# Cross-attention and feed-forward, two layers: four stages run into one another

## What is computed

```
x = x + xattn0(layernorm(x), ctx)          # attention over channels, 32 rows a head
x = x + ffn0(layernorm(x), 4-bit weights)  # silu(gate) * up, down, then y / rms(y)
x = x + xattn1(layernorm(x), ctx)          # 16 heads of 32, below
x = x + ffn1(layernorm(x))                 # ternary weights, gelu between

xattn1: q = x @ Wq + bq;  k, v = split(ctx @ Wkv + bkv)
        q, k, v rounded to 127 steps of their maxima (q, k per row and head, v per column)
        p = softmax(q k^T) over all 2048 keys, rounded to 255 steps of its row maximum
        out = (p v) @ Wp + bp
```

## Time and profile before

| | us |
|---|---|
| median of 3 runs | 1866.02 |
| lowest, highest | 1864.51, 1867.11 |
| the profiled execution | 1868.98 |
| its span in the trace | 1867.2 |

### The profile page before, as it was taken

How to read it: one execution, slowest core, us unless ns; L and a number is a source line. 1 busy time by engine, 2 the same in 40 slices (tenths; PEclk the granted TensorE clock), 3 DMA queues, 4 the chain that set the end, 5 groups by cost and what they waited for, 6 DMA issues and landing times. The chain is left out here.

```text
span 1867.2 us, 30272 instructions
## 1 busy us (share of the span) xinstructions
PE 1699.0 (91%) x10553; PEld 747.7 (40%) x10706; DVE 1494.4 (80%) x2799; ACT 1248.7 (67%) x2107; POOL 907.1 (49%) x927
## 2 busy tenths in 40 slices
PE   3999999689999977989799999999999997999999
PEld 0333233134444433434244444444444444444444
DVE  5899999876867664877699999999999995884332
ACT  4888888445544431223399999999999995774333
POOL 5667665355445420000088888888888884000000
PEclk8999999889999998999899999999999998999999
DMA  9856551301011005556455555655666667110220
GB/s 203 224 147 139 143 145 29 105 11 23 1 23 23 1 6 175 101 101 116 89 108 108 109 109 108 113 109 114 114 114 106 105 108 229 31 23 27 42 45 23
DMA packets 421687, 170.45 MB, mean 91 GB/s; under 512 B 382112, under 2 KB 392352, under 8 KB 420384
## 3 DMA queue, kind: packets, MB, share of 16 engines
q1 hardware_dynamic: 421536, 168.51, 41.8%
HBM read 69.89 MB, written 4.19 MB: 40 GB/s over the span
## 5 line engine op out<-in xcount | busy, mean ns | idle before, releaser
L1586 ACT ACTIVATE a_prob<-a_psS,a_bias,q_scale 128x1024 uint8<-128x1024 f32 x512 | 610.7, 1210 | 25.5 <-PE a_psS L1479 20.5
L1515 DVE TENSOR_REDUCE a_tops<-a_psM 128x1 f32<-128x512 f32 x1024 | 622.7, 681 | 2.0 <-PE a_psM L1469 0.6
L1565 POOL CAST a_wide<-a_pairs 128x2048 int16<-128x2048 uint8 x256 | 481.4, 1891 | 96.9 <-DMA a_pairs<-a_prob 87.8
L1469 PE MATMUL a_psM<-KT,QO 128*128 128x512 bf16 x969 | 354.0, 387 | 21.9 <-DVE a_tops L1515 10.5
L1479 PE MATMUL a_psS<-KT,QO 128*128 128x512 bf16 x966 | 292.6, 380 | 6.7 <-ACT a_prob L1586 3.7
L1491 PEld LDWEIGHTS a_psO<-V,a_wide 128*128 128x128 f16 x4096 | 174.9, 96 | 144.9 <-DVE QO L1528 23.0
L1491 PE MATMUL a_psO<-V,a_wide 128*128 128x32 bf16 x4096 | 181.3, 177 | 20.4 <-DVE QO L1528 15.6
L843 DVE SCALAR_TENSOR_TENSOR g_sum<-g_psG,gu_scale,g_sum 128x512 f32<-128x512 f32 x176 | 124.2, 746 | 89.8 <-PE g_psG L995 75.0
L821 POOL TENSOR_TENSOR g_sum<-g_sum 128x512 f32<-128x512 f32 x88 | 126.3, 1435 | 140.4 <-DVE g_sum L843 140.4
L478 ACT ACTIVATE prob<-psT 128x512 f32<-128x512 f32 x256 | 142.9, 599 | 63.8 <-remote 32.0
L942 ACT ACTIVATE g_sum<-g_psG,gu_scale 128x512 f32<-128x512 f32 x176 | 111.2, 681 | 109.9 <-PE g_psG L995 109.0
(11 more groups left out here) (212 smaller groups left out, 2737.5 us busy)
## 6 DMA issues: line engine op xcount, KB each, us to landing
xs<-in_x SPq DMA_DIRECT2D x64, 256.0 KB, 6.2
cs<-in_ctx SPq DMA_DIRECT2D x64, 256.0 KB, 8.3
KT<-in_w SPq DMA_DIRECT2D x2, 4096.0 KB, 19.1
raw_gu<-in_gu SPq DMA_DIRECT2D x4, 1408.0 KB, 8.1
vs<-in_ctxT SPq DMA_DIRECT2D x16, 256.0 KB, 2.9
QO<-in_ctxT SPq DMA_DIRECT2D x4, 1024.0 KB, 11.3
a_pairs<-a_prob SPq DMA_TRANSPOSE x256, 2.7
out<-x_sb SPq DMA_DIRECT2D x16, 256.0 KB, 2.2
```

The lines of the kernel that those rows point to most:

```text
L1469: pe.matmul(psM[n % NM][:, :], QOf[:, i * P:(i + 1) * P], KTf[:, keys:keys + 512], start=True, stop=True).then_inc(shown, 1)
L1515: v.reduce_max(tops[i // JOIN % NB][:, i % JOIN, c:c + 1], psM[n % NM][:, :], AX.X).then_inc(topped, 1)
L1565: pool.tensor_copy(wide[i % NV][:, :, :, :].rearrange("p k c q -> p k (c q)"), both).then_inc(widened, 1)
L1586: act.activation(prob[i % NP][:, k * HK:(k + 1) * HK], psS[g % NS][:, :], ACT.Exp, scale=q_scale[:, i:i + 1], bias=bias[i // JOIN % NB][:, ...
```

## The change

The gated stage and the keys, values and queries become one block, and so do the attention and the projection with what follows; between these two blocks all engines still meet. Within a block each engine goes on to the next stage's program when its own is through, and waits on semaphores guard memory and banks that are used again.

- A tile `early` of 7 x 512 words a partition takes the first context piece, the value weights of groups 0 and 1, and the key bias. SP issues these three behind the gated stage's transposes. All else it issues after the gated stage's last product, row and copy. The tile later holds the projection's `o` and `oT`.
- The ring of the keys has three banks (NA = 3). `bias_rows(0)` comes first on VectorE, `bias_rows(1)` after value unit 5, the normaliser after unit 7. ScalarE loads its table at the start of this stage.
- From query tile 8 on, TensorE makes two `show` products after each query tile and VectorE takes two maxima, so that the 16 of the first four steps are made in the query stage. Attention's own programs start behind them.
- The factor 1/sqrt(32) is taken into each query tile's operations; the operation on all of q_scale and the one that negates it are gone, and GpSimd negates in its second small operation.
- SP no longer waits for the turned tiles; GpSimd does so before its first `offset`, and TensorE before the tiles it reads.
- In attention `psM` moves behind `psS` and `psO` in PSUM (banks 5 to 7 instead of 0 to 2), and the maxima with what is made of them lie in one tile of 28 words a partition.
- TensorE transposes and projects tiles 0 and 1 between the last four `weigh` steps. VectorE inverts 15 tiles' sums and divides before it copies the last head's result (`keep_last`, after the update of tile 0). The ternary weights are issued when the last score is made.

```diff
+        ffn = gated_ffn(env, dn_in, dns_in)
+        keys = keys_values_queries(env, ctxT_in, wkv_in, bkv_in, bv_in, wq_in, bq_in, ahead)
+        with nc.Block() as block:
+            @block.sync
+            def _(sp):
+                ffn.sync(sp)
+                keys.sync(sp)
...
+        with nc.Block() as block:
+            @block.sync
+            def _(sp):
+                attended.sync(sp)
+                rest.sync(sp)
...
-    NA = 4
-    AHEAD = 4
+    NA, AHEAD, FIRST_SHOWN = 3, 4, 8
...
-            sp.dma_start(bv[:, :], bv_in).then_inc(loaded[0], 16)
-            fetch_wv(0, 0)
+            fetch_wv(wv_first, 0, 0)
             fetch_ctx(0, 0)
-            fetch_wv(1, 1)
+            sp.dma_start(raw[0], bkv_in[0:DM].partition_broadcast(P)).then_inc(loaded[5], 16)
+            for done in ("products", "rows", "taken"):
+                sp.wait_ge(*env["ffn_done"][done])
+            sp.dma_start(bv[:, :], bv_in).then_inc(loaded[1], 16)
             fetch_ctx(1, 2)
...
-            sp.wait_ge(v_turned, 16 * CH)
-            for b in range(2):
-                sp.wait_ge(turned[b], 16 * NT)
...
-            normaliser(v, env)
+            bias_rows(0)
             for kind, i in ORDER:
                 if kind == "v":
                     values(i)
-                    if i == 1:
-                        bias_rows(0)
-                    if i == 3:
+                    if i == 5:
+                        v.wait_ge(b_own, 5)
                         bias_rows(1)
                         v.wait_ge(b_own, 10)
+                    if i == 7:
+                        v.wait_ge(*env["ffn_done"]["stats"])
+                        normaliser(v, env)
...
                     if i + 4 < NT:
                         normalise(i + 4)
+                    if i >= FIRST_SHOWN:
+                        for n in (2 * (i - FIRST_SHOWN), 2 * (i - FIRST_SHOWN) + 1):
+                            piece(v, n // CH, n % CH)
...
+                    if i == FIRST_SHOWN:
+                        pe.wait_ge(turned[0], 16 * (NT // 2 + 1))
+                        pe.wait_ge(turned[1], 16 * NT // 2)
+                    if i >= FIRST_SHOWN:
+                        for n in (2 * (i - FIRST_SHOWN), 2 * (i - FIRST_SHOWN) + 1):
+                            show(pe, n // CH, n % CH)
...
-            for i in range(AHEAD):
-                for c in range(PIECES):
-                    show(i, c)
...
+                if i >= N:
+                    turn(pe, i - N)
...
-            pool.wait_ge(negated, 1)
+            for b in range(2):
+                pool.wait_ge(env["keys_done"]["turned"][b], 16 * NT)
...
+        def turn(pe, i):
+            if i == 0:
+                pe.wait_ge(*env["attended"]["topped"])
+                transpose(pe, 0)
+                transpose(pe, 1)
+            if i == 1:
+                pe.wait_ge(w_in, 16 * (CH + 1))
+                pe.wait_ge(env["attended"]["exped"], 2 * H1 * NT)
+            if i in (1, 2):
+                project(pe, i - 1)
+                transpose(pe, i + 1)
...
+            sp.wait_ge(*env["attended"]["scored"])
             for i, (w_dram, n) in enumerate(((w1_in, FF), (w2_in, DM))):
...
+            v.wait_ge(attended["exped"], 2 * H1 * (NT - 1))
+            v.wait_ge(attended["o_read"][0], NT - 1)
             invert(own, 0, 2)
             divide(0)
             divide(1)
-            invert(own, 2, NT)
+            invert(own, 2, NT - 1)
...
+                if t == 1:
+                    keep_last()
+                    v.wait_ge(attended["exped"], 2 * H1 * NT)
+                    invert(own, NT - 1, NT)
```

More of the change, by code:

```diff
@@ L1 @@
+from collections import namedtuple
 from contextlib import ExitStack
@@ L142, in build @@
         env["w_sums"] = sb("w_sums", [P, 2 * WS], F32)
[L143 to L155, removed]
+        env["V"] = sb("V", [P, NT, H1, D1], BF16)
@@ new lines, in build @@
+        env["v_scale"] = sb("v_scale", [P, CH], F32)
+        env["QO"] = sb("QO", [P, NT * H1, P], BF16)
+        env["q_scale"] = sb("q_scale", [P, NT * H1], F32)
+        env["maxima"] = sb("maxima", [P, 28], F32)
+        env["wp_loaded"] = env["sems"].enter_context(nc.semaphore("wp_loaded"))
+        with ExitStack() as later:
+            env["e_sum"] = later.enter_context(nc.sbuf_tensor("e_sum", [P, NT * H1 * 2], F32))
+            rest, turn = project_and_ternary(env, w1_in, w2_in, b1_in, b2_in, out)
+            attended, ahead = attend(env, wp_in, bp_in, turn)
@@ L779, in gated_ffn @@
              "squared", "own", "added", "after"))
-        block = ctx.enter_context(nc.Block())
+        env["ffn_done"] = dict(products=(y_done, NT), rows=(added, NT), stats=(after_s, NT), taken=(y_taken, NT))
         SIDES = (0, 1)
@@ L1162, in _, with gpsimd @@
                     turn_queries(i)
-            sp.wait_ge(v_turned, 16 * CH)
-            for b in range(2):
-                sp.wait_ge(turned[b], 16 * NT)
-        @block.gpsimd
-        def _(pool):
+        def gpsimd(pool):
+            for done in ("products", "rows", "taken"):
+                pool.wait_ge(*env["ffn_done"][done])
             pool.memset(ones_b[:, :], 1.0).then_inc(blank, 1)
@@ L1353, in keys @@
                 for i in range(CH):
-                    pe.matmul(out[:, :], cT[:, i, t * P:(t + 1) * P], wkv[:, i, 0:DM], start=(i == 0), stop=False)
+                    pe.matmul(out[:, :], context(t // TPC)[:, i, t % TPC * P:(t % TPC + 1) * P], wkv[:, i, 0:DM], start=(i == 0), stop=False)
                 pe.matmul(out[:, :], ones_b[:, :], rows[0][:, :], start=False, stop=True).then_inc(k_done, 1)
@@ L1436, in attend, with show, join, piece @@
         spare = QO[:, :, :].rearrange("p (t h) n -> p t (h n)", h=H1)[:, :, 2 * DM:]
+        env["psO"] = psO
+        env["attended"] = dict(exped=exped, weighed=weighed, topped=(topped, N * PIECES), o_read=(o_read, NT),
+                               scored=(scored, 2 * N))
+        def show(pe, i, c):
+            n = PIECES * i + c
+            if n >= NM:
+                pe.wait_ge(topped, n - NM + 1)
+            keys = (i % H1) * TOK + c * 512
+            pe.matmul(psM[n % NM][:, :], QOf[:, i * P:(i + 1) * P], KTf[:, keys:keys + 512],
+                      start=True, stop=True).then_inc(shown, 1)
+        def join(v, b):
+            v.wait_ge(topped, PIECES * JOIN * (b + 1))
+            if b >= NB:
+                v.wait_ge(lowest, b - NB + 1)
+            v.reduce_max(top[b % NB], tops[b % NB][:, :, :], AX.X).then_inc(joined, 1)
+        def piece(v, i, c):
+            n = PIECES * i + c
+            v.wait_ge(shown, n + 1)
+            v.reduce_max(tops[i // JOIN % NB][:, i % JOIN, c:c + 1], psM[n % NM][:, :], AX.X).then_inc(topped, 1)
+            if c == 0 and i % JOIN == 0 and i:
+                join(v, i // JOIN - 1)
         def landed(i):
             return turned[i % NW], 16 * (i // NW + 1)
-        @block.sync
-        def _(sp):
+        def sync(sp):
             def fetch(c):
@@ L1459, in _, with tensor @@
                     fetch(i // H1 - FIRST_LOAD)
[L1461 to L1470 removed]
+        def tensor(pe):
             def score(i, k):
@@ L1541, in _, with gpsimd @@
                 for c in range(1, PIECES):
-                    piece(i + AHEAD, c)
-            join(N // JOIN - 1)
-            keep(NT - 1)
-        @block.gpsimd
-        def _(pool):
+                    piece(v, i + AHEAD, c)
+            join(v, N // JOIN - 1)
+        def gpsimd(pool):
             def offset(b):
```

301 lines of the change are left out of this document (158 added, 143 removed).

## The result

The changed kernel takes **1838.05 us** (median of 4 runs, 1837.88 to 1838.84) where the kernel before took 1865.72 beside it (4 runs, 1864.51 to 1867.11): ratio 0.9854, 95% interval 0.9841 to 0.9867, or 27.7 us less. Forecast were 1839 and 27 less. The profiled execution took 1837.88 with a span of 1836.1.

The account below looks back on a forecast made before the run. VectorE's row maxima were taken to bound mid-attention, with idle engines at the seams. 17.7 - 7.5 - 3.1 + 10.7 + 9.0 = 26.8 us took the profiled 1868.98 to 1842.2, median 1839; range 1831 to 1849.

Parts of the forecast that it names:

- A: Gated stage to keys: early first fetches let value unit 4 start at 715.8 instead of 733.53, gaining 17.7 us.
- The conversion to the median: Whole kernel: profiled execution, forecast at 1842.2, lies 3.0 us above the median, so the median would become 1839.
- B: Keys: bias row and normaliser moved there delay VectorE, stopping TensorE 5.2 us plus a slow unit; loses 7.5 us.
- absorbed: Rival in the keys: VectorE catches up before a bank is missed, no loss there, 1832 us; chance 0.12.
- two stops: Rival in the keys: backlog costs more, a second half-clock stop, loss near 14 us, 1846 us; chance 0.12.
- C: Query stage: fourteen extra products for maxima on TensorE from query tile 8, 0.22 us each, losing 3.1 us.
- D: Keys to attention: earlier stage end and sixteen reductions and a join less, minus 2 for half-clock start; gains 10.7 us.
- E: Attention joined with projection: first projection products between last heads, product 3 at 1572.9 instead of 1581.9; gains 9.0 us.
- The rival that the projection waits for the weights or runs at half clock: Part of the rival that seams keep their waits, here attention to projection: 1843 to 1848 us; chance 0.15.
- the one without gain at the join: Rival at attention to projection: early projections only delay head 255 and its chain, gain about 2, 1846 us; chance 0.08.
- Slower: Rival in attention: 1008 remaining maxima lengthen with moved banks and results; 27 ns each erases the gain; chance 0.03.
- a reading in which TensorE sets the pace: Attention: sixteen moved products would save only their TensorE spacing, 3.5 us instead of 9.8; no separate chance given.

Follow-up runs that it names:

- the three-bank kernel: The kernel before the change with three banks in the ring of the keys instead of four, nothing else: 1865.99 us, ratio 1.0008.
- after: The changed kernel itself, against the kernel before: 1838.05 us, ratio 0.9854.
- the meeting before the projection: The changed kernel with engines meeting between attention and projection, all projection transposes and products behind that: 1845.21 us (median of three), ratio 0.989.
- the long execution: Profiled execution of the changed kernel with normaliser and second bias row early, seven redundant products before value unit 2, key tile 15 before query transposes: median 1831.02 us.
- the yardstick: The changed kernel with the normaliser after value unit 1 and second bias row after unit 3, rerun on another chip: 1829.33 us, ratio 0.9795.

## Why the prediction was right

**A, +17.7 forecast.** Unit 4 was to start at 715.8 and started at 712.80. The gated stage ended 0.4 earlier. The transfer took 5.1 from issue to use, not 6.7. I took the old first piece's 7.2 less a little; but with the same weights ahead of it that piece took 5.3 in the three-bank kernel's trace, so 7.2 belonged to one execution and was not the price of what stood ahead. And the slow stretch was 9.25 for two units, 0.9 less than 6.7 + 3.43. Against the profiled execution that is +20.7. Against the other execution of the old seam it is 42.7 less 25.6, or 17.1.

**The conversion to the median** was the step that was wrong in kind. I took 3.0 off the forecast because the profiled execution lay 3.0 above the median, as if that excess were spread over stages that stay. As far as the two traces of the old seam show, most of it sat in the seam that was removed. The right reckoning leaves it out of A and out of the conversion. I was 3.0 too low on A by the trace and took off 3.0 that had gone with it, and the two cancelled: that 1839 came within 1 of 1838.05 is in this part luck. By the rests, from the three-bank kernel's 1176.0 to 1148.9 is 27.1, for a forecast sum of 26.8 and a median difference of 27.7; with the traced execution's own 1179.6 it is 30.7.

**B, -7.5 forecast, -8.0 seen.** Starts of VectorE on key tiles 2, 3 and 4 were to lie 2.5, 4.3 and 10.4 behind TensorE and lay 2.4, 4.2 and 10.3 behind. The stop was 5.02 for a forecast 5.2, and the slow unit cost 2.85 over its 3.60, not 2.3. Both rivals on the backlog (absorbed, or two stops) fall.

**C, -3.1 forecast, -2.7 seen**, with query steps of 4.5 from tile 8 on.

**D, +10.7 forecast, +11.5 seen.** First exponential at 8.5 as said. The half-clock start cost about 1 where I charged 2: VectorE waited 0.35 and 0.42 for products and was then again the pace. The part of D that the earlier end of the block gives (2.9 forecast) was not undone by itself.

**E, +9.0 forecast, +9.0 seen**, undone at a cost of 7.2 by the median and 9.1 by the rest. Product 2 of the projection was to start about 5 behind the last widening and started 4.4 behind it (1541.67 to 1546.03). Product 0 was not slow (3.67). The rival that the projection waits for the weights or runs at half clock falls with it, as does the one without gain at the join. Part of this too is luck: I had costed VectorE's operations on the sums and rows at their old durations, and they took some 8 us more beside GpSimd (last section), which happened to lie under TensorE's weighings and product 0.

**Slower.** The reductions of the attention took 681 ns in the mean before and after, so moving their banks and results cost nothing.

**What paces the attention.** By a reading in which TensorE sets the pace, the sixteen maxima were worth 3.5 us there, and putting them back would have cost 0.8 after the 2.7 that the query stage saves. It cost 7.1: VectorE sets the pace, and 92% busy on TensorE was not the bound. The Trainium skill ("Trainium Kernel Development and Optimization", Performance Expectations, on reading a trace) warns that matmul busy time is a bad measure; the trace agrees.

## What to carry over

A seam is worth more than its wait: the gaps of 5 us and more in these seams also made the next products slow, so 5 us of waiting cost 8. When work is moved into another engine's idle time, follow that engine's queue to the tile that its user needs next; the same 4.4 us cost nothing behind value unit 1 and 7 behind unit 7. And if the profiled execution lies above its median, look for where, before taking the difference off a forecast. Measuring from the last point that the edit can't touch leaves out what an execution lost before it, but it rests on one trace and is read beside the median, not in its place.

## What the runs showed of the hardware

**VectorE beside GpSimd.** VectorE's first small operations on the sums, at the attention's end, in after:

```profile
1526.34 1.13 DVE L1795 TENSOR_TENSOR e_sum<-e_sum 128x32 f32<-128x32 f32 x1
1527.51 1.79 DVE L1796 TENSOR_SCALAR e_sum<-e_sum 128x32 f32<-128x32 f32 x1
...
1529.73 2.99 DVE L1803 TENSOR_TENSOR early<-QO,e_sum 128x512 f32<-128x512 f32 x2
...
1536.61 1.45 DVE L1797 RECIPROCAL e_sum<-e_sum 128x208 f32<-128x208 f32 x1
```

and with the meeting before the projection, where GpSimd has ended:

```profile
1541.36 0.20 DVE L1809 TENSOR_TENSOR e_sum<-e_sum 128x32 f32<-128x32 f32 x1 [15.79 <-PEq L187]
1541.58 0.18 DVE L1810 TENSOR_SCALAR e_sum<-e_sum 128x32 f32<-128x32 f32 x1
...
1542.19 1.29 DVE L1817 TENSOR_TENSOR early<-QO,e_sum 128x512 f32<-128x512 f32 x2
...
1544.11 1.46 DVE L1811 RECIPROCAL e_sum<-e_sum 128x208 f32<-128x208 f32 x1
```

GpSimd's widenings in after's trace, 1.9 us each when nothing holds them up:

```profile
1525.54 3.73 POOL L1633 CAST a_wide<-a_pairs 128x2048 int16<-128x2048 uint8 x2
```

The first two of VectorE's operations end at 1527.47 and 1529.30, each within 0.1 us of the end of a widening (1527.43 and 1529.27): they end with the widening that runs beside them, and so 0.18 us becomes 1.79. The reciprocal over 208 columns takes 1.45 and 1.46, though it overlaps the widening that starts at 1536.88, and the reductions out of PSUM stay at 681 ns. It goes the other way too: the widening that starts at 1529.78, just behind VectorE's operation of 1529.73, takes 2.39.

This fits the Trainium skill's "SBUF — State Buffer" (SBUF: two separate sides): VectorE and GpSimd share one pair of ports, and whoever starts first holds it for its whole instruction, against VectorE operations in a two-port mode or with two inputs in SBUF.

It also fits the unpackings of 0.57 and 1.51 us. Here is one of each with GpSimd's instruction beside it, first in the long execution, then in the yardstick:

```profile
186.55 1.16 POOL L447 TENSOR_TENSOR ks<-cs,k_sub 128x512 f16<-128x512 f32 x1
186.58 1.51 DVE L790 TENSOR_SCALAR raw_gu<-raw_gu,shift 128x704 int32<-128x704 int32 x1
```

```profile
184.06 2.64 POOL L447 TENSOR_TENSOR ks<-cs,k_sub 128x512 f16<-128x512 f32 x2
185.12 0.57 DVE L790 TENSOR_SCALAR raw_gu<-raw_gu,shift 128x704 int32<-128x704 int32 x1
```

In the long execution the unpacking starts 0.03 us behind the start of a GpSimd instruction and is held up. In the yardstick it starts 1.06 behind one of 1.16, and now the next GpSimd instruction takes 1.52 instead of 1.16. So it is with this operation in all six rounds from 180 to 300 us of both traces. No run moved the one against the other on purpose, and what sets the order of their starts in an execution stays open.

**The clock.** It was 0.50 after a wait of only 2.69 us at the first seam, and stayed at 1.00 when redundant products closed it. Behind the wait of 0.68 us before value unit 9 that unit took 3.70 instead of 3.60. So half-filling a gap can leave the whole of what it costs.
